# A macaron transformer layer in f32: router logits from unnormalised rows, taken in the last attention group, with the norm weight folded into the expert weights

## What is computed

```python
x = x + 0.5 * _L0_ffn_ref(_layernorm(x), ...)
x = x + _L0_attn_ref(_layernorm(x), ...)
x = x + 0.5 * _L0_ffn_ref(_layernorm(x), ...)

# _L0_ffn_ref: causal attention with 16 heads of 8, then a mixture of 8 experts, top 2
h = _rmsnorm(x, ln1_w)
...
x = x + ao @ wo
h = _rmsnorm(x, ln2_w)                      # x * rsqrt(mean(x*x) + eps) * ln2_w
logits = h @ router_w
probs = softmax(logits)
topv, topi = top_k(probs, 2); topv = topv / sum(topv)
gate, up = h @ w_gate[e], h @ w_up[e]       # 128 -> 448 for each expert e
moe = (silu(gate) * up * weights) @ w_down[e]
return x + moe
```

## Time and profile before

| | us |
|---|---|
| median of 3 runs | 1901.65 |
| fastest, slowest of these | 1900.51, 1904.47 |
| the profiled execution | 1902.52 |
| its span, first to last instruction | 1900.9 |

### The profile page before, as it was taken

One profiled execution on the slowest core, in us unless ns is written; L12 is line 12 of the kernel. 1 busy time (PEld: TensorE's weight loads), 2 busy tenths in 40 slices (PEclk: granted clock), 3 DMA queues, 4 the chain that ended last, 5 costly groups with the idle time before them and its releaser, 6 DMA issues. The chain is left out here.

```text
span 1900.9 us, 30318 instructions
## 1 busy us (share of the span) xinstructions
PE 1678.3 (88%) x10566; PEld 720.8 (38%) x10566; DVE 1379.6 (73%) x2863; ACT 1073.4 (56%) x2301; POOL 444.9 (23%) x492
## 2 busy tenths in 40 slices
PE   4799999999749948899999999579999999993995
PEld 2333333333237723233333332233333333323674
DVE  8788899987153348888999983388899999826333
ACT  2355677677614413356777678234576777781442
POOL 6300201111016637000102020260011010200664
PEclk9788999999859967889999999678899999995898
DMA  4500203300011134200202000242002020001113
GB/s 130 118 21 3 51 3 99 71 2 2 8 33 41 43 103 139 52 1 2 52 2 52 3 2 2 60 139 52 2 12 42 2 52 2 2 2 30 38 43 88
DMA packets 63574, 75.83 MB, mean 40 GB/s; under 512 B 13655, under 2 KB 56220, under 8 KB 62104
## 3 DMA queue, kind: packets, MB, share of 16 engines
q1 hardware_dynamic: 54184, 62.13, 13.1%
q0 software_dynamic: 4992, 9.40, 2.0%
q10 hardware_dynamic: 4224, 2.10, 0.4%
HBM read 53.05 MB, written 21.46 MB: 39 GB/s over the span
## 5 line engine op out<-in xcount | busy, mean ns | idle before, releaser
L753 ACT ACTIVATE probs<-ps 128x512 f32<-128x512 f32 (+3 forms) x1920 | 879.1, 542 | 473.0 <-PE ps L861 471.6
L604 DVE TENSOR_REDUCE mpart<-ps 128x1 f32<-128x512 f32 (+3 forms) x1680 | 1015.1, 666 | 117.3 <-PE ps L815 65.5
L815 PE MATMUL ps<-ka,qa 96*128 96x512 bf16 (+3 forms) x1920 | 669.9, 371 | 36.4 <-DMA ka<-ksplit 23.6
L861 PE MATMUL ps<-qa,ka 96*128 96x512 bf16 (+3 forms) x1920 | 616.1, 357 | 3.1 <-DMA qa<-guard 2.5
L874 PE MATMUL ps<-probs,vv 128*9 128x512 f32 (+3 forms) x3840 | 441.8, 532 | 8.8 <-ACT probs L753 8.1
L702 POOL TENSOR_SCALAR_AFFINE_SELECT probs<-probs 128x512 f32<-128x512 f32 x192 | 121.8, 634 | 1180.0 <-ACT probs L753 1180.0
L815 PEld LDWEIGHTS ps<-ka,qa 96*128 96x128 bf16 x1920 | 191.9, 100 | 480.7 <-DVE mpart L604 338.6
L861 PEld LDWEIGHTS ps<-qa,ka 96*128 96x128 bf16 x1920 | 183.6, 100 | 189.0 <-ACT probs L753 69.2
L818 PE MATMUL ps<-mask_rows,identb 128*128 128x128 bf16 x768 | 161.4, 235 | 0.0
L1212 DVE SCALAR_TENSOR_TENSOR probs<-probs,slot_w,ps 128x448 f32<-128x448 f32 x78 | 53.1, 680 | 117.2 <-PE ps L1133 113.7
L874 PEld LDWEIGHTS ps<-probs,vv 128*9 128x9 f32 x3840 | 57.7, 88 | 157.8 <-ACT probs L753 116.4
(11 more groups left out here) (170 smaller groups left out, 1092.8 us busy)
## 6 DMA issues: line engine op xcount, KB each, us to landing
qa<-qsplit SPq DMA_DIRECT2D x27, 384.0 KB
ka<-ksplit SPq DMA_DIRECT2D x27, 384.0 KB
probs<-rope SPq DMA_DIRECT2D x12, 512.0 KB, 6.7
qa<-qsplit SPq DMA_DIRECT2D x36, 96.0 KB
ka<-ksplit SPq DMA_DIRECT2D x36, 96.0 KB
qsplit<-arena SPq DMA_DIRECT2D x6, 384.0 KB, 3.2
ksplit<-arena SPq DMA_DIRECT2D x6, 384.0 KB, 2.8
tokens<-arena SPq DMA_DIRECT2D x2, 1024.0 KB, 7.4
```

The source lines that it names most:

```text
L604: dve.tensor_reduce(mpart[:, j % MD, h0:h0 + some, qt, kc], ps[:, bank, 0:some * w].rearrange("p (h w) -> p h w", h=some), axis=AX.X, op=A ...
L753: act.activation(probs[:, s % 2, h, 0:n], ps[:, u % SB, 0:n], ACT.Exp, scale=SCALE).then_inc(probs_ready, 1)
L815: ins = pe.matmul(dst, qa[0:KROWS, b, h0 + k, tile * 128:(tile + 1) * 128], ka[0:KROWS, b, h0 + k, kc * CH:kc * CH + n], start=True, stop= ...
L861: pe.matmul(dst, ka[0:KROWS, b, h, kt * 128:(kt + 1) * 128], qa[0:KROWS, b, h, c * CH + q0:(c + 1) * CH], start=True, stop=True).then_inc( ...
```

## The change

It has these parts, all in one diff. The router takes its logits from the unnormalised `x1` rows: since the norm is one positive factor a token, the order of the experts does not depend on it, and only the gap between the two best logits is multiplied by it afterwards. The weight `ln2_w` is multiplied into `rts`, `wgs` and `wus` once, by POOL, in layer 0. For chunks 0 to 2 of each layer, transposes ("relay") and logits become fillers of the last attention group, in all three layers; only chunk 3 is left in the router stage. The 16 `h2` rows are made by ACT. POOL's `x1` rows move to a later place, and the guard memsets are moved from before the loop into each layer. Token rows in DRAM are numbered 16 p + t in place of 128 t + p, with the two weights in the same line, so that one partition's rows are one run.

```diff
@@ -72,7 +72,8 @@
         nonlocal pe, dve
         kind, j, at = late.pop(0)
         pe = max(pe, at, banks[bank]) + (900 if kind == "project" else 450)
-        dve = max(dve, pe + hop) + {"normalise": 500, "turn": 650, "project": 2600}[kind]
+        dve = max(dve, pe + hop) + {"normalise": 500, "turn": 650, "project": 2600, "relay": 700,
         events.append((kind, j))
...
             late.insert(0, ("project", c, dve + hop))
+        elif kind == "project" and c < NC - 1:
+            late.insert(0, ("relay", c, dve + hop))
+        elif kind == "relay":
...
 
-    h2 = arena[:, 0:T].rearrange("p (t d) -> p t d", d=D)
-    moves = arena[:, T:T + NK * NSLOT // 2].bitcast(F16).rearrange("p (k u) -> p k u", k=NK)
-    xr0 = T + NK * NSLOT // 2
+    h2 = arena[:, 0:TT * (D + TOPK)].rearrange("p (t d) -> p t d", d=D + TOPK)
+    top_w = h2[:, :, D:D + TOPK]
+    mv0 = TT * (D + TOPK)
+    moves = arena[:, mv0:mv0 + NK * NSLOT // 2].bitcast(F16).rearrange("p (k u) -> p k u", k=NK)
+    xr0 = mv0 + NK * NSLOT // 2
...
-            pool.memset(key_guard(1), ONES).then_inc(pool_s, 1)
-            pool.wait_ge(pool_s, 1)
-            n = 1
+            n = 0
...
-            pool.iota(inti[:, NSLOT + TT:NSLOT + 2 * TT], pattern=[[128, TT]], base=1, channel_multiplier=1).then_inc(pool_s, 1)
-            pool.iota(inti[:, NSLOT + 2 * TT:NSLOT + 3 * TT], pattern=[[-128, TT]], base=-1,
-                      channel_multiplier=-1).then_inc(pool_s, 1)
+            pool.iota(inti[:, NSLOT + TT:NSLOT + 2 * TT], pattern=[[1, TT]], base=1, channel_multiplier=TT).then_inc(pool_s, 1)
+            pool.iota(inti[:, NSLOT + 2 * TT:NSLOT + 3 * TT], pattern=[[-1, TT]], base=-1,
+                      channel_multiplier=-TT).then_inc(pool_s, 1)
...
-
-            dve.memset(key_guard(0), ONES).then_inc(dve_s, 1)
...
+                    if c == 1:
+                        sp.wait_ge(keys_guarded, 1)
...
+                            loaded = weights_loaded if j > BULK else router_loaded
                             with sp.If(layer == 0):
-                                sp.dma_start(dst, src).then_inc(weights_loaded, 16)
+                                sp.dma_start(dst, src).then_inc(loaded, 16)
...
+                sp.wait_ge(weights_scaled, 3)
...
                         dve.wait_ge(squares_done, TPC * (c + 1))
+                    elif kind == "relay":
+                        c = ev[1]
+                        dve.tensor_copy(hT[:, c * CH:(c + 1) * CH], ps[:, bank, :]).then_inc(filler_used, 1)
+                    elif kind == "logits":
+                        c = ev[1]
+                        dve.tensor_copy(logits[:, TPC * c:TPC * (c + 1), :],
+                                        ps[:, bank, 0:TPC * E].rearrange("p (t e) -> p t e", e=E)
...
@@ -685,16 +705,36 @@
                 third(2 * NC - 2)
                 third(2 * NC - 1)
 
+                pool.wait_ge(part2_ready, 2 * NC)
+                pool.memset(key_guard(1), ONES).then_inc(keys_guarded, 1)
+                pool.wait_ge(keys_guarded, 2)
+                pool.memset(guard_rows(1), 0.0).then_inc(guard_zeroed, 1)
+                pool.wait_ge(guard_zeroed, 1)
+
                 for i in (3, 4):
                     pool.wait_ge(parts_stored[i % PB], stored(i))
                 pool.wait_ge(part2_ready, 2 * NC)
                 pool.wait_ge(roots_ready, 1)
-                for t in range(TT):
-                    pool.tensor_scalar(x1[:, t, :], xs[:, t, :], mv[:, t, 0:1], rst[:, 0, t:t + 1],
-                                       ALU.subtract, ALU.mult).then_inc(x1_ready, 1)
                 for ev in events:
                     if ev[0] == "scores":
+                        if j == NC - 1 and kt == 0 and h == 0:
+                            for t in range(TT):
+                                pool.tensor_scalar(x1[:, t, :], xs[:, t, :], mv[:, t, 0:1], rst[:, 0, t:t + 1],
+                                                   ALU.subtract, ALU.mult).then_inc(x1_ready, 1)
+                        if j == (NG - 1) * NC and kt == 0 and h == 0:
+                            with pool.If(layer == 0):
+                                pool.wait_ge(router_loaded, 16)
+                                pool.tensor_scalar(rts[:, :], rts[:, :], b4s[:, C_LN2:C_LN2 + 1], None,
+                                                   ALU.mult).then_inc(weights_scaled, 1)
+                                pool.wait_ge(weights_scaled, 1)
+                        if j == (NG - 1) * NC + 2 and kt == 0 and h == 0:
+                            with pool.If(layer == 0):
+                                pool.wait_ge(weights_loaded, 48)
+                                for k, w in enumerate((wgs, wus)):
+                                    pool.tensor_scalar(w[:, :, :], w[:, :, :], b4s[:, C_LN2:C_LN2 + 1], None,
+                                                       ALU.mult).then_inc(weights_scaled, 1)
+                                    pool.wait_ge(weights_scaled, k + 2)
...
+                    elif kind == "relay":
+
+                        c = ev[1]
+                        pe.wait_ge(residual_added, c + 1)
+                        for k in range(TPC):
+                            ins = pe.transpose(ps[:, bank, k * 128:(k + 1) * 128], x1[:, TPC * c + k, :], identf[:, :])
+                        ins.then_inc(filler_ready, 1)
+                        written = mi
+                    elif kind == "logits":
+                        c = ev[1]
+                        pe.wait_ge(filler_used, written)
+                        pe.wait_ge(weights_scaled, 1)
+                        for k in range(TPC):
+                            t = TPC * c + k
+                            ins = pe.matmul(ps[:, bank, k * E:(k + 1) * E], hT[:, t * 128:(t + 1) * 128], rts[:, :],
+                                            start=True, stop=True)
+                        ins.then_inc(filler_ready, 1)
...
+                    pe.wait_ge(residual_added, NC)
+                    for k in range(TPC):
+                        t = TPC * (NC - 1) + k
+                        ins = pe.transpose(ps[:, 4, k * 128:(k + 1) * 128], x1[:, t, :], identf[:, :])
+                    ins.then_inc(h2_turned, 1)
+                    pe.wait_ge(h2_copied, 1)
+                    for k in range(TPC):
+                        t = TPC * (NC - 1) + k
+                        ins = pe.matmul(ps[:, 6, k * E:(k + 1) * E], hT[:, t * 128:(t + 1) * 128], rts[:, :],
+                                        start=True, stop=True)
+                    ins.then_inc(logits_ready, 1)
...
-                    for c in range(NC):
-                        act.wait_ge(h2_turned, c + 1)
-                        act.activation(hT[:, c * CH:(c + 1) * CH], ps[:, 4 + c % 2, :], ACT.Copy).then_inc(h2_copied, 1)
+                    act.wait_ge(inverse_ready, 1)
+                    for t in range(TT):
+                        act.activation(h2[:, t, 0:D], x1[:, t, :], ACT.Copy,
+                                       scale=rst[:, 3, t:t + 1]).then_inc(h2_ready, 1)
...
+                    dve.wait_ge(h2_turned, 1)
+                    dve.tensor_copy(hT[:, (NC - 1) * CH:T], ps[:, 4, :]).then_inc(h2_copied, 1)
                     dve.wait_ge(root_ready, 1)
-                    link(dve.reciprocal(rst[:, 3, :], rst[:, 2, :]))
-                    for t in range(TT):
-                        dve.scalar_tensor_tensor(h2[:, t, :], x1[:, t, :], rst[:, 3, t:t + 1], vbc[:, V_LN2, :],
-                                                 ALU.mult, ALU.mult).then_inc(h2_ready, 1)
-                    dve.wait_ge(logits_ready, NC)
-                    lg = ps[:, 6, 0:TT * E].rearrange("p (t e) -> p t e", e=E)
+                    dve.reciprocal(rst[:, 3, :], rst[:, 2, :]).then_inc(inverse_ready, 1)
+                    dve.wait_ge(filler_used, fillers)
+                    dve.wait_ge(logits_ready, 1)
+                    lg = logits[:, :, :]
+                    link(dve.tensor_copy(lg[:, TPC * (NC - 1):TT, :], ps[:, 6, 0:TPC * E].rearrange("p (t e) -> p t e", e=E)))
...
-                    dve.tensor_tensor(gs[:, 5, :], gs[:, 4, :], gs[:, 2, :], ALU.subtract).then_inc(gap_ready, 1)
+                    link(dve.tensor_tensor(gs[:, 5, :], gs[:, 4, :], gs[:, 2, :], ALU.subtract))
+                    dve.wait_ge(inverse_ready, 1)
+                    dve.tensor_tensor(gs[:, 5, :], gs[:, 5, :], rst[:, 3, :], ALU.mult).then_inc(gap_ready, 1)
...
                     sp.wait_ge(h2_ready, TT)
-                    rows = tokens.rearrange("(t p) d -> p t d", p=128)
-                    sp.dma_start(rows[:, :, 0:D], h2).then_inc(tokens_stored, 16)
                     sp.wait_ge(weights_ready, 1)
-                    sp.dma_start(rows[:, :, D:D + TOPK], top_w[:, :, :]).then_inc(tokens_stored, 16)
-                    sp.wait_ge(tokens_stored, 32)
+                    sp.dma_start(tokens.rearrange("(p t) d -> p t d", p=128), h2).then_inc(tokens_stored, 16)
```

(5 more changed lines are left out.)

58 lines of the change are left out of this document (24 added, 34 removed).

## The result

| | us |
|---|---|
| kernel before, median of 7 runs | 1900.55 |
| changed kernel, median of 7 runs | 1907.65 (1905.48 to 1911.98) |
| ratio of the two, 95% interval | 1.0031 (1.0017 to 1.0046) |
| spans of the profiled executions, before and after | 1900.9, 1906.1 |

The change made the kernel about 0.3% slower; the forecast was a gain of 10.5 us. The stages that lose are found with the timeline: the starts of certain instructions are read in both traces, and the distances between them are compared. The table does that at the borders of the stages. "First DVE row" is the first of the layer, "router" DVE's first row of the router stage, "gather" POOL's first indirect DMA, "results" the first load of results on SP's queue.

A forecast was written before the change was run, and what follows sets the result against it. Attention was taken as a full machine with PE and ACT level, the router stage as a one-engine-at-a-time chain. Terms -3.5 - 16.6 - 1.2 + 10.8 = -10.5 took 1901.65 to 1891.2 us, range 1884 to 1900.

The forecast's parts named there:

- POOL (taken at nothing): POOL's moved `x1` rows, guard memsets and layer 0 weight scaling, at most 10.8 us a tile, stay hidden: 0 us.
- Rows numbered by partition: Results loads after the experts: longer lines make the first landing sooner, -0.6 us each, -1.2 in all.
- Before the loop: Start of kernel: without the `ka` memset DVE starts its row statistics sooner, -3.5 us.
- Router stage: Layers 0 and 2: only chunk 3 left before the pick, -8.3 us a layer, -16.6 for two.
- Fillers: Last attention group: relay and logits on PE cost 3.6 us a layer, +10.8 for three.
- Rivals 1: Last attention group: fillers find slack, only chunk 15 pays, +4 in place of +10.8, 1884.4 us; chance 0.12.
- Rival 3: Last attention group: every filler stalls on its handover, +26 in place of +10.8, 1906.6 us; chance 0.06.
- Rival 2: Layer 0, chunk 14: scaling makes POOL's masks late, +17.5 (1908.7 us) or half the excess, +8 (1899); chance 0.08 each.
- rival 4: Whole kernel: late gap exponential, results no sooner, fillers 5 us a layer; -2.5 together, 1899.2 us; chance 0.05.

The follow-up runs named there:

- e7: Kernel before with only the token rows numbered by partition; 1903.47 us, ratio 1.0012 to the kernel before.
- e6: Kernel before with only the moved guard memsets and POOL's moved `x1` rows; 1919.19 us against 1923.15 on that chip, ratio 0.9978.
- e3: Changed kernel with POOL's two whole scalings of `wgs` and `wus` (and the small one of `rts`) moved earlier, to chunk 11; 1892.07 us, ratio 0.9953 to the kernel before.
- e3b: The same kernel as e3, measured once more; 1893.25 us, ratio 0.9963 to the kernel before.
- e11: Changed kernel with DVE row statistics (one SBUF input) in place of the last group's squares; 1894.92 us, ratio 0.9965 to the kernel before.
- e5: Kernel before with only POOL's two scalings added, by ones, in chunk 14 of layer 0; 1935.06 us against 1923.15 on that chip, ratio 1.0069.
- e8: e3 plus a wait: POOL adds each results chunk only after DVE has added the previous one; ratio 0.9957 to the kernel before.
- e9: e3 without the relay and logits fillers, all four chunks done in the router stage; ratio 0.9956 to the kernel before.

## Why the prediction was wrong

- **The step that failed is "POOL (taken at nothing)".** It priced the scaling well (at most 10.8 us a tile; 9.35 and 9.45 measured, while the 5.4 us estimated from the Trainium skill were too few) and found it a window between two masks, and the rival built on it asked only whether POOL would be late for its own work. It never asked what DVE reads while POOL holds SBUF. Both sides of the clash stand in the trace of the kernel before. At the start of the loop a 128x16 operation of DVE, with one input, takes 3.46 us beside POOL's memset at 14.15, and POOL's second addition in the tail, shown above, takes 1.64 us in place of 1.26 beside DVE's:

```profile
14.23 3.46 DVE L549 TENSOR_SCALAR rst<-mv 128x16 f32<-128x16 f32 x1 [1.69 <-PEq L464]
457.10 0.29 DVE L664 CUSTOM_DVE_ANT_0 rec<-x 128x128 f32<-128x128 f32 x1
...
457.75 0.28 DVE L664 CUSTOM_DVE_ANT_0 rec<-x 128x128 f32<-128x128 f32 x1
```

  The last two rows are the first and the fourth square of the same chunk before the change. Two tiles of their measured length, laid behind the mask that ends at 448.0, meet at 457.4, among these squares; at the forecast's 10.8 us a tile they meet at 458.8, with the squares in the last two microseconds of the first. So the danger could be read there, and its size hung on a microsecond of placing. The runs put the cost at 13.2 us: 8.2 of waiting on DVE, 8.7 by the time that ACT has its next bank, and 4.5 more at the lower clock behind it. The Trainium skill (SBUF — State Buffer, section "Who interferes with whom") states that a VectorE instruction with two SBUF inputs contends with a GpSimd instruction that reads SBUF, and that issue order decides who blocks. These traces agree, with 8.46 us for 0.29 where POOL came first, and 1.64 for 1.26 on POOL where DVE did. By that rule the scaling had to be placed against DVE's rows. A stall of 8 us alone would have brought the sum from -10.5 to about -2.
- **Rows numbered by partition: sign wrong.** -0.6 a tail was forecast, +2.7 and +2.5 were measured in the changed kernel, +1.5 and +1.4 in e7. The sentence "only the first landing is on the path" held only for the old spacing of the landings. The first landing came no sooner, and the next ones came so close that POOL's additions started ahead of DVE's and held them.
- **Before the loop: right.** -3.5 forecast, -4.0 measured (14.23 to 10.24; -4.03 in e6), inside its bounds.
- **Router stage: right.** -8.3 forecast (8.7 less 0.3 is 8.4, a slip of 0.1), -8.49 and -8.46 measured. The pick starts 4.19 us after the router's first row, as said (about 4), and the table load ends at 540.19, just before the exponential at 540.36, so the moved activations cost nothing. It was close: the margin is 0.17 us, the 16 took 4.78 us and not 4.4, and 0.1 us more for each of them would have cost about 1.4 us, not 0.7:

```profile
531.94 1.28 ACT L970 ACT_TABLE_LOAD   x1 [8.89 <-PEq L476]
533.23 0.21 ACT L970 ACTIVATE rst<-rst 128x16 f32<-128x16 f32 x1
534.11 4.78 ACT L973 ACTIVATE arena<-x,rst 128x128 f32<-128x128 f32 x16 [0.67 <-DVE rst L992]
538.91 1.28 ACT L976 ACT_TABLE_LOAD   x1
540.36 0.22 ACT L976 ACTIVATE gs<-gs 128x16 f32<-128x16 f32 x1 [0.17 <-DVE gs L1017]
```

- **Fillers: right.** 3.6 us a layer forecast; 3.78 in layer 0's stretch, and 3.68 and 3.78 by the same chunks of layers 1 and 2. Pricing them by `project` worked; whether row maxima slid into slack, as the forecast has it for 0.4 us, was not tested. Rivals 1 and 3 are out. (Rival 3's time should read 1906.4: 26 in place of 10.8 on 1891.2.)
- **Rival 2** is out: no mask waited for POOL. The measured time lies near its 1908.7, but by another mechanism. Of **rival 4**'s ends only one came, the results landing no sooner.
- With the scaling placed elsewhere the sum holds, by luck in part: e3's span is 10.5 us under before (by the medians e3 gains 9.9 and e3b 8.2). The terms as measured give -4.0 - 17.0 + 11.2 + 5.2 (tails) = -4.6, the experts' stages give another -1.95, and the rest of e3's gain lies in the stages that vary by themselves. Why the experts' stages are 0.7 to 1.1 us shorter in the changed kernels of the table and not in e7 (127.75, 127.61) stayed open.

## What to carry to other kernels

Before a long instruction is put on GpSimd, list what VectorE does in those microseconds: with two inputs in SBUF it stands until GpSimd lets go, and everything queued behind it stands as well. Cut the GpSimd work into pieces of about a microsecond, or put it where VectorE reads PSUM or one SBUF tensor; either gave back the 13 us here. And when a faster transfer feeds a pair of engines that add in turn, look at which of them will start first once the pieces come closer together.

## What the runs showed of the hardware

- POOL holds VectorE for less than its recorded row (or the row ends late). The addition issued 8.15 us into the 9.35 us tile was late by only 0.17 us, at 451.82, 1.0 before the tile's recorded end; the square issued 0.25 us into the 9.45 us tile came free 8.2 us later, 1.0 us before that tile's recorded end.
- The price on POOL of a tensor_scalar with one operation: 9.35 us for 3584 columns and 1.39 for 448, so 2.5 ns a column and 0.25 us fixed. By that, 128 columns are 0.57 us; the row of 791 ns, with two operations and two operands, lies above it and would have misled by its price a column (6.2 ns).
- A VectorE operation with one SBUF input can be held too. At the loop's start a 128x16 tensor_scalar takes 3.46 us beside POOL's memset of 3.50, where the like of it takes 0.18 in the router stage (the kernel before has the same row, at 14.23):

```profile
10.24 3.46 DVE L561 TENSOR_SCALAR rst<-mv 128x16 f32<-128x16 f32 x1 [1.71 <-PEq L472]
```

```profile
10.16 3.50 POOL L691 MEMSET ka<- 32x4096 f32 x1 [2.01 <-POOL qa L457]
```

  The statistics of e11 passed. No run here tells which operations with one input are held.
- On the chip that ran e5, e6, e8 and e9 the experts' stage took 136 to 139 us in kernels of both kinds, against 127 on the others, and the stages of the table that do not vary by themselves were the same within 0.6 us of kernels with the same work. Why is open; the ratios compare kernels on one chip.
